# Two more units by seven products in the second layer, and lo of three units kept in DRAM

## The reference

```
# layer 1
out = (adj / (rowsum(adj) + 1e-5)) @ x @ W_neigh.T + b_neigh + x @ W_self.T + b_self
x   = layernorm(x + relu(out))
# layer 2, d = rowsum(adj) ** -0.5
out = (d[:, None] * adj * d[None, :]) @ x @ W + b
x   = layernorm(x + relu(out))
```

## Time and profile before

| | us |
|---|---|
| median of 3 runs | 776.36 (775.98 to 776.51) |
| the profiled execution | 776.1 |
| its span, from first to last instruction | 774.4 |
| PE busy | 766.6 (99%) |
| PE weight loads busy | 662.6 (86%) |
| DVE busy | 720.0 (93%) |
| ACT busy | 429.5 (55%) |
| DMA queues q1 and q10, share of 16 engines | 59.6% |

### The profile page before, as it was taken

The page is one execution under the profiler, slowest core; times in us unless marked ns, Lnnn a source line. Parts: engine busy times, 40 slices in busy tenths (PEclk is TensorE's granted clock), DMA queues, the critical chain, the costliest instruction groups (busy, mean ns, idle before and its releaser), DMA issues.

```text
span 774.4 us, 12666 instructions
## 1 busy us (share of the span) xinstructions
PE 766.6 (99%) x4151; PEld 662.6 (86%) x4151; DVE 720.0 (93%) x1226; ACT 429.5 (55%) x594; POOL 2.5 (0%) x14
## 2 busy tenths in 40 slices
PE   9999999999999999999999999999999999999996
PEld 6888888888888888888888889899898989989896
DVE  6999999999899899998989899898989989898996
ACT  5644645646446364454554755665565566656663
POOL 0000000000000000000000000000000000000000
PEclk9999999999999999999999999999999999999999
DMA  7975574655646547474574756656565665756651
GB/s 302 346 237 195 191 264 155 243 187 200 234 154 244 189 168 266 135 267 168 176 260 147 243 178 208 216 195 241 172 228 198 215 217 176 257 165 229 204 190 61
DMA packets 54206, 161.09 MB, mean 208 GB/s; under 512 B 5024, under 2 KB 18080, under 8 KB 54176
## 3 DMA queue, kind: packets, MB, share of 16 engines
q1 hardware_dynamic: 45680, 151.54, 55.9%
q10 hardware_dynamic: 8352, 9.05, 3.7%
q0 software_dynamic: 144, 0.13, 0.2%
HBM read 152.31 MB, written 8.39 MB: 208 GB/s over the span
## 4 chain that ended last, share of the span: by engine, by line
PE 98%; DVE 1%; ACT 1%; issue 0%; ACTq 0%
PE ps_main L1100 72%; PE ps_epi L979 7%; PE ps_epi L1047 7%; PE ps_main L1038 4%; PE ps_main L1047 2%; PE ps_epi L1038 2%; PE ps_main L979 1%; PE ps_main L1075 1%; PE ps_main L1122 1%; PE ps_main L1060 1%; PE ps_epi L1132 0%; ACT hi L359 0%; ACT xt_sb L382 0%; ACT tt L406 0%; DVE tt L618 0%; PE ps_epi L1000 0%
## 5 line engine op out<-in xcount | busy, mean ns | idle before, releaser
L359 ACT ACTIVATE hi<-raw 128x1024 fp32r<-128x1024 f32 x254 | 254.9, 1013 | 134.5 <-PE ps_main L1100 86.9
L562 DVE TENSOR_TENSOR lo<-raw,hi 128x1024 fp32r<-128x1024 f32 x254 | 296.7, 1170 | 22.5 <-ACT hi L359 22.0
L1100 PE MATMUL ps_main<-hi,xs 128*128 128x512 f32 x1120 | 278.8, 391 | 0.0
L1100 PEld LDWEIGHTS ps_main<-hi,xs 128*128 128x128 f32 x1120 | 207.4, 188 | 41.7 <-issue 0.5
L1100 PE MATMUL ps_main<-lo,xs 128*128 128x512 f32 x560 | 149.7, 389 | 0.0
L853 DVE TENSOR_TENSOR acc<-acc,raw 128x1024 f32<-128x1024 f32 x112 | 136.4, 1218 | 0.0
L1100 PE MATMUL ps_main<-hi,zs 128*128 128x512 f32 x504 | 125.6, 391 | 0.0
L1100 PEld LDWEIGHTS ps_main<-lo,xs 128*128 128x128 f32 x560 | 105.1, 188 | 21.9
L1100 PEld LDWEIGHTS ps_main<-hi,zs 128*128 128x128 f32 x504 | 92.2, 188 | 17.6
L359 ACT ACTIVATE xs<-acc 128x1024 fp32r<-128x1024 f32 (+1 forms) x52 | 54.6, 1050 | 69.3 <-DVE acc L746 55.8
L1047 PE MATMUL ps_epi<-xs 128*128 128x256 f32 x423 | 69.7, 283 | 0.0
(11 more groups left out here) (158 smaller groups left out, 814.8 us busy)
## 6 DMA issues: line engine op xcount, KB each, us to landing
raw<-adj_t SPq DMA_DIRECT2D x256, 512.0 KB, 3.3
res<-x_nat SPq DMA_DIRECT2D x11, 512.0 KB, 5.3
xt_sb<-xt SPq DMA_DIRECT2D x8, 512.0 KB, 5.1
x_scratch<-tt ACTq DMA_DIRECT2D x8, 512.0 KB, 3.8
res<-x_scratch SPq DMA_DIRECT2D x8, 512.0 KB, 4.8
out<-tt ACTq DMA_DIRECT2D x7, 512.0 KB, 4.9
tt<-x_nat SPq DMA_DIRECT2D x3, 512.0 KB, 4.7
acc<-x_nat ACTq DMA_DIRECT2D x1, 512.0 KB, 5.0
```

The costliest lines, as they stand in the source:

```text
L359: return act.activation(dst, src, ACT.Copy)
L562: return dve.tensor_tensor(dst, src, hi_part.bitcast(f32), ALU.subtract)
L1100: last = pe.matmul(ps[:, f, :], stationary(layer, part, jt, f), mov[:, slot(u), cols], start=(jt == 0 and i == 0), stop=(jt == JT - 1 and ...
```

## The change

- `SU` has nine units, 1, 2, 5, 6, 7, 9, 11, 12, 13, for blocks 1 to 6; block 7 keeps its five (`SU_LAST`), and block 0 has none.
- There are five groups of T, and a new place in `T_UNITS` at unit 2 of block 0. T takes four more tiles of `xs`, so the third place of the ring of split sums moves to the weights of the first layer (`wn`, `ws`), which the second layer does not use.
- The first layer stores lo of units 4, 8 and 10 of blocks 1 to 6 into DRAM (`lo_dram`), four units later, behind the load into the same slot. DVE waits for that store before it writes the slot again.
- In the second layer SP loads them back into their slots of `lo`, once ACT has split the unit. DVE does a memset of one column in place of the subtraction, and PE waits for the load (`lo_full`).
- The sums of unit 2 are made at unit 1, those of others two units ahead as before; `slot_taken` is worked out anew, and tells whether the sums come behind `s_lo` of the unit at hand.

```diff
-SU = (1, 5, 7, 9, 11, 12, 13)
+SU = (1, 2, 5, 6, 7, 9, 11, 12, 13)
+SU_LAST = (1, 5, 7, 9, 11)
+KEPT = (4, 8, 10)
-T_UNITS = (4, 6, 9, 11)
+T_UNITS = (2, 4, 6, 9, 11)
...
+        def lead(v):
+            return 1 if v == 2 else max(v - 2, 0)
+        def s_place(b, u):
+            return by_seven(1, b).index(u)
...
+        def s_part(part, b, u):
+            s = s_place(b, u) % SRING
+            if s == SRING - 1:
+                return (wn, ws)[part][:, :, :, :].rearrange("p a k f -> p (a k f)")
+            at = S_AT + s * 4 + part * 2
             return xs[:, at:at + 2].rearrange("p a c f -> p (a c f)")
...
+                    if layer == 0 and u - RING in kept(b):
+                        sp.dma_start(lo_dram[b, KEPT.index(u - RING)], lo[:, slot(u), :].bitcast(f32))\
+                          .then_inc(lo_stored[slot(u)], 16)
...
+                    if layer == 1 and u - RING + 1 in kept(b):
+                        v = u - RING + 1
+                        sp.wait_ge(h_ready, g0 + (v + 1))
+                        sp.dma_start(lo[:, slot(v), :].bitcast(f32), lo_dram[b, KEPT.index(v)])\
+                          .then_inc(lo_full[slot(v)], 16)
...
-                        split_lo(lo[:, slot(u), cols], raw[:, slot(u), cols], hi[:, slot(u), cols]).then_inc(l_ready, 1)
+                        if layer == 0 and u - RING in kept(b):
+                            dve.wait_ge(lo_stored[slot(u)], kept_count(b, u - RING))
+                        if layer == 1 and u in kept(b):
+                            dve.memset(marks[:, 2:3], 0.0).then_inc(l_ready, 1)
+                        else:
+                            split_lo(lo[:, slot(u), cols], raw[:, slot(u), cols], hi[:, slot(u), cols])\
+                                .then_inc(l_ready, 1)
                     place(u, 1)
                     if by_seven(layer, b):
-                        ahead = [v for v in by_seven(layer, b) if max(v - 2, 0) == u]
-                        slot_taken = u in SU and u + 1 in SU
+                        units = by_seven(layer, b)
+                        ahead = [v for v in units if lead(v) == u]
+                        slot_taken = ahead and len([v for v in units if u <= v < ahead[0]]) == 2
...
-                        if i == 2:
+                        if i == 2 and layer == 1 and u in kept(b):
+                            pe.wait_ge(lo_full[slot(u)], kept_count(b, u))
+                        elif i == 2:
                             pe.wait_ge(l_ready, g0 + (u + 1))
```

More of the change, by code:

```diff
@@ L42 @@
 WARM = 10
-SU = (1, 5, 7, 9, 11, 12, 13)
+SU = (1, 2, 5, 6, 7, 9, 11, 12, 13)
+SU_LAST = (1, 5, 7, 9, 11)
 NS = len(SU)
 SRING = 3
+KEPT = (4, 8, 10)
+NK = len(KEPT)
 T_AT = XC + FH
-T_UNITS = (4, 6, 9, 11)
+T_UNITS = (2, 4, 6, 9, 11)
 S_AT = T_AT + 2 * NS
@@ L72, in build @@
         x1_dram = nc.dram_tensor("x1_scratch", [NB, TB, P, F], f32, kind="Internal").ap()
+        lo_dram = nc.dram_tensor("lo_scratch", [NB, NK, P, UW], f32, kind="Internal").ap()
         xs = sb("xs", [P, JT, 2, F], f32r)
@@ L129, in build @@
         tt_stored = sem("tt_stored")
+        lo_stored = [sem(f"lo_stored{s}") for s in range(RING)]
+        lo_full = [sem(f"lo_full{s}") for s in range(RING)]
         ones_set = sem("ones_set")
@@ L194, in by_seven, with kept, kept_in_slot, kept_count @@
                 return ()
-            return tuple(u for u in SU if u < TAIL) if is_last(b) else SU
+            return SU_LAST if is_last(b) else SU
+        def kept(b):
+            return () if isinstance(b, int) else KEPT
+        def kept_in_slot(u):
+            return [v for v in KEPT if slot(v) == slot(u)]
+        def kept_count(b, u):
+            per_block = len(kept_in_slot(u))
+            return (b * per_block + (kept_in_slot(u).index(u) + 1 - per_block)) * 16
+        def lead(v):
+            return 1 if v == 2 else max(v - 2, 0)
+        def s_place(b, u):
+            return by_seven(1, b).index(u)
         def tile_sums(layer, e, parity, t):
@@ L209, in s_index, with s_sums_of, s_sum @@
         def s_index(b, u):
[L211 to L223, removed]
+            return b * NS + (s_place(b, u) - NS)
+        def s_sums_of(b, parity, u):
+            return acc[:, (s_place(b, u) + NS * (1 - parity)) % 2, :]
+        def s_sum(b, parity, u, i):
+            return s_sums_of(b, parity, u)[:, i * HB:(i + 1) * HB]
+        def s_part(part, b, u):
[3 more added lines that the diff above has]
+            at = S_AT + s * 4 + part * 2
             return xs[:, at:at + 2].rearrange("p a c f -> p (a c f)")
@@ L303, in one_block @@
                     sp.dma_start(raw[:, slot(u), :], adj_in[b, u]).then_inc(raw_full[slot(u)], 16)
+                    if layer == 0 and u - RING in kept(b):
+                        sp.dma_start(lo_dram[b, KEPT.index(u - RING)], lo[:, slot(u), :].bitcast(f32))\
+                          .then_inc(lo_stored[slot(u)], 16)
+                    if layer == 1 and is_first(b) and u == NU - 1:
+                        for v in KEPT:
+                            sp.wait_ge(lo_stored[slot(v)], len(kept_in_slot(v)) * (NB - 2) * 16)
+                    if layer == 1 and u - RING + 1 in kept(b):
[3 more added lines that the diff above has]
+                          .then_inc(lo_full[slot(v)], 16)
                     if layer == 0:
@@ L392, in s_hi @@
                 act.wait_ge(s_ready, s_index(b, u) + 1)
-                split_hi(s_part(0, u), s_sums_of(parity, u)).then_inc(sh_ready, 1)
+                split_hi(s_part(0, b, u), s_sums_of(b, parity, u)).then_inc(sh_ready, 1)
             def square_tiles(layer, e, parity, pair):
@@ L734, in s_sums @@
                 _, a22, a11, a21 = [raw[:, slot(u), i * HB:(i + 1) * HB] for i in range(4)]
-                s1, s2, s3 = [s_sum(parity, u, i) for i in range(3)]
-                if SU.index(u) >= 2:
+                s1, s2, s3 = [s_sum(b, parity, u, i) for i in range(3)]
+                if s_place(b, u) >= 2:
                     dve.wait_ge(sl_ready, g - 1)
@@ L745, in s_last_sum @@
                 dve.wait_ge(s_chain, s_index(b, u) * 3 + 3)
-                dve.tensor_tensor(s_sum(parity, u, 3), raw[:, slot(u), 0:HB], s_sum(parity, u, 1), ALU.subtract)\
+                dve.tensor_tensor(s_sum(b, parity, u, 3), raw[:, slot(u), 0:HB], s_sum(b, parity, u, 1), ALU.subtract)\
                     .then_inc(s_ready, 1)
@@ L750, in s_lo @@
                 dve.wait_ge(sh_ready, s_index(b, u) + 1)
-                split_lo(s_part(1, u), s_sums_of(parity, u), s_part(0, u)).then_inc(sl_ready, 1)
+                split_lo(s_part(1, b, u), s_sums_of(b, parity, u), s_part(0, b, u)).then_inc(sl_ready, 1)
             def epilogue(layer, e, parity, v, p):
@@ L1044, in seven_products @@
                         pe.wait_ge(sl_ready, s + 1)
-                    mov = s_part((0, 0, 1)[i], u)
+                    mov = s_part((0, 0, 1)[i], b, u)
                     for n, (ps, st, at) in enumerate(summed):
```

## The result

| | before | after |
|---|---|---|
| median, us (5 runs each) | 776.39 (775.98 to 776.91) | 784.59 (783.52 to 786.19) |
| ratio | | 1.0107, 95% interval 1.0093 to 1.0121 |
| the profiled execution, its span | 776.1, 774.4 | 786.19, 784.5 |

The change makes the kernel 8.2 us slower. The profiled execution is the slowest of the five, and 1.5 of its 10.1 us arise ahead of the blocks that the change touches, near the start: the second block's row sums of PE into ps_epi are at 110.50 in place of 109.00, and at 43.99 PE had waited 0.46 us for DVE, as it did not before. Where tenths count I use that one.

The account below looks back on a forecast made before the run. DVE's closed loop with ACT was taken to set the pace: block 0's 1.0 plus 6 x 1.15 gives 7.9, less 0.37 is +7.5 us, on 776.1 783.6, as a median 783.9; range 779.5 to 787.5.

Parts of the forecast that it names:

- The closed loop: Second-layer blocks: DVE waits for ACT, which waits for DVE's nmr, so added DVE work lengthens the period to 46.54 us.
- Rival A: Second-layer blocks: PE stays the bound, DVE's idle 3.2 us a block takes the added 1.15; 773.7 us, chance 0.10.
- rival B: Second-layer blocks: DVE's period grows by less than its lead over PE can bear; 776.4 us, chance 0.04.
- D: Rival: nothing is absorbed, all new DVE work in block 0 and six blocks adds 12.8 us; 789 us, chance 0.06.
- One sign named for "wrong": Second-layer blocks: PE stopped before the last third of unit 4 by lo_full would point to the late reload, rival C.
- The terms of the sum: DVE's work per second-layer block: units 1 to 3 +1.81, 4 to 6 +1.48, 8 and 10 -2.14, sum +1.15 us.
- The memset: DVE's one-column stand-in for a kept lo's subtraction: costed at 0.07 us, bounds 0 and 0.3, no such memset in the trace.
- Block 0: Second layer's first block, with a fifth group of T: DVE leaves it about 1.0 us late (0.6 to 1.4).
- path (b): Kernel's end by DVE and ACT: a 7.9 us shift less a 0.37 wait for PE gives +7.5 us, the path that counts.
- PE's path by the reload: Block 6, unit 4: reload landing after 3.3 us makes PE 6.4 late, 7.4 behind a raw load, just under path (b).
- rival C: Second-layer reload lands late and stops PE at unit 4, deciding from about 4.4 us; 784.6 to 788.4 us, chance 0.12.
- The stores: First layer: 18 stores of 512 KB costed at nothing; if their cover goes, at most 3.3 us each.

Follow-up runs that it names:

- g1: Changed kernel with first two norms later except in the last block, reload one unit earlier, units 0, 4, 8 and 10 kept: 775.32 us, ratio 0.9981 to before.
- e3: Changed kernel with each kept lo asked back one unit earlier on SyncE: 783.24 us, ratio 1.0083 to the kernel before.
- e0: The changed kernel itself, run again beside other kernels: 784.86 us, ratio 1.0102 to the kernel before.
- e1: Changed kernel without store and reload, so DVE makes lo of units 4, 8 and 10 itself: 804.73 us, ratio 1.0360 to the kernel before.
- e6: Changed kernel with ScalarE's first two norms in the second layer moved behind hi of unit 15: 781.06 us, ratio 1.0047 to the kernel before.
- e8: Changed kernel with the first two norms later, reload one unit earlier, and units 3, 4, 8 and 10 kept: 780.35 us, ratio 1.0038 to before.

## Why the prediction was right

783.9 was forecast, 784.59 measured. The mechanism is the one named; the closeness is luck in part, since two sizes were off in opposite directions.

**The closed loop: right.** PE's 0.45 us a block was saved (0.42 by g1) and bought nothing, DVE's idle time stayed where it was, the period grew by the added work, and PE takes 46.45 - 44.70 = 1.75 us a block more than it needs (1.8 predicted). The windows show only 0.54 and 1.07 of that as idle time; as in e3, a stop can cost more than its bracket. Rival A is excluded by the period, rival B by the time, and D by 46.43 (its 1.49 a block would have made it 46.9). One sign named for "wrong" did appear: lo_full stopped PE ahead of the last third of unit 4. e3 shows that in blocks 2 to 5 this was a place where PE met DVE's delay, not the cause.

**The terms of the sum.** In block 3, against the same rows before, in the profile after: lo of unit 3 comes 10.68 us behind lo of unit 0, before 8.93, so units 1 to 3 cost +1.75 (predicted 1.81); up to the row behind unit 6 it is 22.00 against 18.80, so units 4 to 6 +1.45 (1.48); to nmr 41.17 against 40.17, so units 8 and 10 -2.20 (-2.14); and to the next lo of unit 0 46.27 against 45.28. Sum +1.00 for 1.15: three small errors of one sign. The memset is one of them:

```profile
567.47 0.17 DVE L681 TENSOR_SCALAR nmean<-sums 128x2 f32<-128x2 f32 x1
567.49 0.06 DVE L868 MEMSET marks<- 128x1 f32 x1
567.58 0.42 DVE L675 SCALAR_TENSOR_TENSOR tt<-tt,res 128x256 f32<-128x256 f32 x1
```

It takes 0.04 us of the queue (0.11 from nmean to the next row, where it was 0.07 before), for which I had 0.07. The prediction says that the trace before has no such memset; it has one, of marks, at 1.43 us, printed at 0.06, far under the 0.3 that bounded the range. The estimated 0.06 us by the Trainium skill ("VectorE: DVE Perf Modes", "The TRN2 errata") agrees with the printed length, and is above what the queue paid.

**Block 0: nearly right.** 1.0 predicted. PE is 1.00 late behind it in e0 (459.48 against 458.48), DVE 1.20 (lo of unit 15 at 441.68 against 440.48). How PE comes by its 1.00 was not foreseen: at 441.46 it is 0.06 late, then it waits 0.83 us for xs of DVE. Where DVE sets the pace this is of no consequence; where PE does, as in g1, it is the 1.0 that is lost.

**The end: the step that failed.** "It does not pass path (b), just", said of PE's path by the reload, was wrong. Path (b) itself came out at 6.97 (e3) for 7.5: 0.9 less by the smaller period (6 x 0.15), 0.1 less by block 0, and some 0.4 more by a raw block that came late in block 1 of e3 too (DVE waited 0.34 us for it). But the reload of unit 4 in block 6 was asked for at 690.59 in e0 and let PE on at 695.39, 4.8 us later and not 3.3 or 4.3, beyond the 4.4 from which rival C was to decide; and a raw block came later in block 1. Together 1.6 us by the medians of e0 and e3. So 0.9 too much for the period stood against 0.3 too little for the rest of path (b) and 1.6 for the reload: 783.9 - 0.9 + 0.3 + 1.6 = 784.9, which is e0's 784.86, though the kernel before was 0.6 us slower in that job too (777.0); the result's 784.59 is within the spread of its five runs. Rival C is true as a second cause of a fifth of the loss, and I had it at 0.12.

**The stores: right.** The first layer's ordinary blocks take 49.58 us as before, with 18 stores of 4.9 us each among the loads.

## What to carry to other kernels

Idle time of a busy engine is spare only if what it waits for does not wait for this engine. Follow the wait back one full turn: if it returns to the engine, added work lengthens the period, by as much of it as fills no wait on the way, and removed work shortens it only where it doesn't cover a shorter wait. Ask of each instruction that you delete what another engine does meanwhile; lo of unit 3 cost 1.22 us of busy time and nothing of the period. And a faster bound engine needs the second one faster too: here the same saving on PE was worth +8.2 us alone and -1.3 us once DVE's loop had been cut in two places.

## What the runs showed of the hardware

Without reloads the raw loads of 512 KB landed in 3.3 us in the median. With three or four reloads a block, and the stores, they took 3.6 to 4.1 us and the reloads themselves 4.1 to 4.8, at a DMA share of 0.69 to 0.79 in a block of the second layer instead of 0.60 to 0.63. The start can differ between executions of one kernel: PE's wait at 43.99 in the profile after is absent in e0, where the same matmuls come at 42.81 and the span is 1.3 us shorter. In the other profiles they come between 42.69 and 44.51, with the wait in e1, e6 and e8. Why is open.
